# Where the second product stands in a feed-forward slot, on VectorE and on TensorE

## The reference

```python
def _qlinear(x, W, b):
    y = q_acc(jnp.einsum('bsk,nk->bsn', q_mul(x), q_mul(W)))
    return q_acc(y + q_mul(b))
h = jax.nn.relu(_qlinear(x, W1, b1))
y = _qlinear(h, W2, b2)
...
t = t + _L0_ffn_ref(_ln_t(t), L0_ffn_W1, L0_ffn_b1, L0_ffn_W2, L0_ffn_b2)
x = _from_tokens(t, x)
x = x + _L1_conv_ref(_ln_c(x), ...
```

## Time and profile before

| what | value |
|---|---|
| runs, median (lowest to highest) | 3300.53 us (3293.03 to 3302.36), 3 runs |
| the profiled execution, its span | 3289.15 us, 3287.5 us |
| TensorE matmuls busy | 2827.3 us, 86% |
| VectorE busy | 2666.6 us, 81% |
| ScalarE busy | 2259.9 us, 69% |
| GpSimd busy | 1862.1 us, 57% |

### The profile page before, as it was taken

How to read it: one execution, slowest core, us unless ns; L and a number is a source line. 1 busy time by engine, 2 the same in 40 slices (tenths; PEclk the granted TensorE clock), 3 DMA queues, 4 the chain that set the end, 5 groups by cost and what they waited for, 6 DMA issues and landing times. The chain is left out here.

```text
span 3287.5 us, 65685 instructions
## 1 busy us (share of the span) xinstructions
PE 2827.3 (86%) x20846; PEld 1472.8 (45%) x20846; DVE 2666.6 (81%) x4380; ACT 2259.9 (69%) x4205; POOL 1862.1 (57%) x1466
## 2 busy tenths in 40 slices
PE   8999989688999999999996679789989779688876
PEld 5666654233444444444432224344334334577732
DVE  6888869537999999999999948679999968444468
ACT  5666658578999899989884428576666458444455
POOL 2333323156889898989897635357777745100046
PEclk9999999899999999999999999899999889899999
DMA  2000001257474747474746123201111022310023
GB/s 88 0 0 0 0 11 46 79 162 198 122 218 133 227 142 221 142 224 140 226 123 173 53 73 90 62 21 26 24 24 24 17 60 90 122 23 22 22 72 78
DMA packets 201533, 294.28 MB, mean 90 GB/s; under 512 B 62242, under 2 KB 179158, under 8 KB 201110
## 3 DMA queue, kind: packets, MB, share of 16 engines
q1 hardware_dynamic: 198678, 288.03, 30.6%
q10 hardware_dynamic: 2688, 4.29, 0.4%
HBM read 190.11 MB, written 102.09 MB: 89 GB/s over the span
## 5 line engine op out<-in xcount | busy, mean ns | idle before, releaser
L1793 POOL TENSOR_TENSOR mam_hc<-mam_h,mam_cs 128x896 f32<-128x896 f32 x336 | 704.4, 2096 | 150.4 <-DVE mam_h L1712 83.8
L1712 DVE TENSOR_TENSOR_SCAN mam_h<-mam_a,mam_kept,mam_dbx 128x448 f32<-128x448 f32 x672 | 737.3, 1126 | 27.3 <-ACT mam_a L1582 26.2
L1435 PE MATMUL mam_ps_y<-mam_hc,mam_ident 128*128 128x448 f32 x1344 | 565.8, 554 | 124.6 <-POOL mam_hc L1793 124.3
L1582 ACT ACTIVATE mam_a<-mam_ft,mam_a_neg 128x448 f32<-128x448 f32 x672 | 409.5, 657 | 77.6 <-DVE mam_h L1712 76.3
L1435 PEld LDWEIGHTS mam_ps_y<-mam_hc,mam_ident 128*128 128x128 f32 x1344 | 246.3, 191 | 422.6 <-POOL mam_hc L1793 215.1
L1699 DVE TENSOR_TENSOR mam_dbx<-mam_ps_u,mam_bs 128x448 f32<-128x448 f32 x672 | 380.3, 609 | 0.0
L682 POOL TENSOR_TENSOR att_prob<-att_prob,att_share 128x588 f32<-128x588 f32 x128 | 149.2, 1188 | 306.2 <-DVE att_share L974 306.2
L2222 POOL TENSOR_TENSOR scan_ch<-scan_h,scan_cs 128x392 f32<-128x392 f32 x192 | 264.4, 1391 | 56.3 <-DVE scan_h L2163 53.9
L368 POOL MEMSET f_squares_ln<- 128x392 f32 x4 | 1.7, 425 | 366.9 <-POOLq L2296 327.3
L387 POOL CAST f_h<-f_hr 128x392 fp8e5<-128x392 f16 x128 | 65.5, 512 | 235.2 <-DVE f_hr L308 235.2
L2163 DVE TENSOR_TENSOR_SCAN scan_h<-scan_decay_by_column,scan_h,scan_drive_by_column 128x392 f32<-128x392 f32 x112 | 197.2, 1760 | 0.0
(11 more groups left out here) (240 smaller groups left out, 6639.2 us busy)
## 6 DMA issues: line engine op xcount, KB each, us to landing
mam_taps<-normed SPq DMA_DIRECT2D x220, 130.5 KB
mam_bs<-dram_bc SPq DMA_DIRECT2D x56, 448.0 KB, 8.2
mam_cs<-dram_bc SPq DMA_DIRECT2D x56, 448.0 KB, 11.2
normed<-f_staged SPq DMA_DIRECT2D x96, 203.0 KB
mam_ft<-dram_steps SPq DMA_DIRECT2D x42, 448.0 KB, 4.8
f_mixed<-mixed SPq DMA_DIRECT2D x64, 196.0 KB, 2.4
mam_gt<-dram_gs SPq DMA_DIRECT2D x48, 224.0 KB, 2.7
dram_gs<-mam_gs SPq DMA_DIRECT2D x47, 224.0 KB, 3.3
```

What stands on the lines that cost most here:

```text
L1435: mm = pe.matmul(ps_y[p % 2][:, 0:MT], ident[:], hc[t % 2][:, i, :], start=False, stop=(t % 8 == 7 and i == 1))
L1582: act.activation(a[t % 3][:, i, :], ft[p % 2][:, 0, :], ACT.Exp, scale=a_neg[:, at:at + 1]).then_inc(decays, 1)
L1712: dve.tensor_tensor_scan(h[:, n % 8, :], a[t % 3][:, i, :], dbx[:, i, 0:MT], kept[:, at:at + 1], ALU.mult, ALU.add).then_inc(scanned, 1)
L1793: pool.tensor_tensor(hc[t % 2][:], h[:, row:row + 2, :], cs[:, 2 * pair:2 * pair + 2, :], ALU.mult).then_inc(weighed, 1)
```

## The change

On VectorE `round_result` becomes the first step of a slot; before, it came fourth. On TensorE `second_product` is given ahead of `hidden_units`. No step is added or dropped, and what each waits for is unchanged.

```diff
                 def slot(s, turn, u, on):
+                    if on[2]:
+                        round_result(s - 2)
                     if on[1]:
                         round_third(s - 1)
                     if on[0]:
                         quantize(s, u)
                     if on[1]:
                         rectify_third(s - 1)
-                    if on[2]:
-                        round_result(s - 2)
-                    if on[1]:
                         rectify(s - 1, 0)
                     if on[2]:
                         add_bias(s - 2)
...
                 def slot(s, turn, u, on):
+                    if on[2]:
+                        second_product(s - 2, u % 2)
                     if on[1]:
                         hidden_units(s - 1)
-                    if on[2]:
-                        second_product(s - 2, u % 2)
                     if not last and on[3]:
                         subtract_mean(ln, "ln", nb, "updated", "normed", s - 3, u)
```

## The result

The changed kernel takes 3357.45 us (median of 4 runs, 3354.45 to 3362.64), against 3299.01 before (4 runs, 3293.03 to 3302.36). The ratio is 1.0182 with a 95% interval of 1.0165 to 1.0200, so it is 58 us slower, four times the forecast of +14.7.

What follows compares the result with a forecast made beforehand. Norm's lap was taken to bound layers 0 to 2, a lap through GpSimd the last layer. The last layer's +17.4 and the others' -2.7 gave +14.7 us on the median 3300.53: 3315.2 us, range 3306 to 3323.

Steps and rivals of the forecast that it cites:

- less the 0.48 of L324, which has left, so 3.18: VectorE's stretch from L295's start to L318's end: 3.66 us before, taken as 3.18 once L324 moves ahead of it.
- the norm loop: Layers 0 to 2: lap from norm through f_xc_ln, square, variance, logarithm and root to norm; 4.53 us, setting today's slots.
- The sentence on L387: GpSimd's L387 would start some 0.48 us later in the slot and still end before L318 does.
- rival C: Last layer: TensorE's clock falls, doubling matmul times in 38% of the time; 13.9 us, net +28.6, chance 0.05.
- Of these 0.10 I take 0.07 off the lap: 4.46.: Layers 0 to 2: the variance, freed from waiting for L324, starts sooner after the square, shortening norm's lap to 4.46 us.
- The prediction's other figure, 142.3 for each: Layers 0 to 2 if the 0.07 is not won: slots stay 4.59 us, +1.1 instead of -2.7, +18.5 in all.
- the rounding loop: Every layer: VectorE's L324 waits for TensorE's second product, which waits for the previous slot's L318; 4.49 us a lap.
- A: Layers 0 to 2 repay more, running at the floor: -8.2 us there, net +9.2, 3309.7 us; chance 0.22.
- B: Layers 0 to 2: the hidden units delay f_xc_ln, so norm's lap grows: +9.4 us, net +26.8, 3327.3 us; chance 0.10.
- D: L324 finds its sum ready, so only the shortening counts: last layer -7.4 us, net -15.6, 3284.9 us; chance 0.03.

Runs made afterwards that it cites:

- last_filled: The changed kernel with one extra matmul of zeros a slot in the last layer, GpSimd's cast left whole; 3349.17 us.
- small_cast_filled: The changed kernel with GpSimd's cast cut to 8 of 392 columns and one extra matmul of zeros a slot in the last layer; 3326.98 us.
- after: The changed kernel itself, both moves in all layers, against the kernel before; 3357.45 us.
- last_as_before: The changed kernel with the old order put back on both engines in the last layer; 3323.58 us.
- held_update: The changed kernel, but GpSimd's update of x waits in every layer until both L301 of the slot are done; 3305.13 us.

## Why the prediction was wrong

The direction and the main mechanism were right, the size was not. By the spans of L318, forecast 562.4 us for the four layers together, measured 606.6. The three steps between, each a difference of two kernels:

- *"... less the 0.48 of L324, which has left, so 3.18."* This step failed: the stretch takes 3.44 in the changed kernel. It took away L324 and kept the durations of the rest. But L324 was also what stood beside GpSimd's cast; without it L330 comes 0.48 earlier and meets the cast, and takes 0.26 more. `last_filled` less `small_cast_filled`, 597.8 less 570.9, is **26.9 us**; 0.27 a slot in the last layer, 0.20 in the others, where the norm loop hides a part of it. The sentence on L387 ("still ends before L318 does") asked only who waits for the cast, not what runs beside it.
- *The clock (rival C, 0.05).* It was priced at 13.9 us and given too small a chance. `after` less `last_filled` in the last layer is 158.1 less 149.3, **8.8 us**; the filling's own 0.65 us makes that some 9.5. The three matmuls of a group do not quite double, 1.14 for 0.66. `last_as_before` and `held_update`, whose slots are shorter there, keep the clock at 1.00, so this cost appeared only with the longer slots.
- *"Of these 0.10 I take 0.07 off the lap: 4.46."* Wrong: the variance starts 0.15 after the square in both kernels. The 0.05 that was set against this 0.15 is the time to a weight load and not to a matmul; the variance's own weight load comes 0.11 after its square before (545.18 to 545.29) and 0.12 after it now (543.91 to 544.03). The weights of f_var_ff do load while the matmuls ahead of them still run, but there was nothing to win by it here. Layers 0 to 2 stayed at the norm loop's 4.53 to 4.70 once the cast was out of the way, 141.9, 143.4 and 144.8 us in `small_cast_filled` instead of 141.05. The prediction's other figure, 142.3 for each, was the nearer one. With 1.6 us more in the last layer that is the remaining **8.5 us**.

Right: the rounding loop. Its parts gave 4.49, 4.71, 4.97 and 4.14 us for four kernels, and the slots were 4.50, 4.71, 4.97 and 4.15. Only the 4.49 was forecast from the kernel before alone, and it came true where the cast had been taken away; the 4.71 and 4.14 use the lengths of L330 and L318 that the runs had shown. Right too: the last layer pays most, because norm does not fill the wait there, and f_ps_y's variance is released by the square. The rivals A, B and D did not come; C came, beside the larger cost that no rival named.

The hint was in the earlier trace rows: L318's shortest is 562 ns and its median 1166, with one form. Two durations of one form mean that something else decides which. L318's own hold was the same in both kernels and so did no harm to the sum, but the question of its cause might have led to L330.

The Trainium skill, "SBUF — State Buffer", section "Who interferes with whom", says that VectorE and GpSimd share one pair of SBUF ports under an exclusive lock, which VectorE's copies, casts and scalar operations need in their fast modes. The traces agree in both directions: 0.57 for 0.31, 1.17 for 0.56, and GpSimd's 1.25 for 0.94.

## What to carry to other kernels

When an instruction is moved, ask what it stood beside, not only what it waits for: an instruction that reads PSUM, set beside GpSimd's work, may be the only thing that keeps two engines out of each other's way. Before using a duration in a sum, compare its shortest and its median in the row; a factor of two there can be a wait hidden inside the instruction. And before a consumer is put first in an in-order queue, check that its producer does not wait for the end of the round before: here it closed a loop of two engines, and its length became the length of the slot.

## What the runs showed of the hardware

- VectorE and GpSimd meet not only at semaphores, as the first section has it: one can be held by the other in the middle of its work, with no semaphore between them.
- A VectorE instruction held by GpSimd shows no idle time; its duration grows. L330 ended 0.12 us after the cast (544.50 to 544.62), and L318 0.43 after the update (544.70 + 0.93 to 544.89 + 1.17). Total busy time then counts waits: the changed kernel's VectorE was busier by 36.5 us with the same instructions.
- GpSimd waits as well: the update took 1.25 us behind L318 in place of 0.94, and the cast 0.84 in place of 0.53.
- VectorE instructions that read f32 from PSUM were not held: in the kernel before, L295 starts at 3202.89, in the middle of L374 (3202.51 to 3203.85), and takes 0.55 us, as it does alone. Whether the PSUM or the type decides is not shown, since all of them here have both.
- TensorE's clock stayed at 1.00 with 85.41 of 120 us busy in `held_update`'s last layer, and was 0.85 with 101.22 of 155 in the changed kernel's. With one matmul of zeros a slot it was 1.00 from 3190 to 3330, in slots as long as the changed kernel's short ones.
- Not every overlap costs. In the kernel before, L301 starts at 545.06, 0.18 ahead of the cast's end, and takes 0.31. It too ends 0.13 after the cast, so it comes too late to lose anything by the hold.
